# Throw-away 512-column matmuls ahead of each tile's scores in three attention stages of a fused decoder kernel

## What is computed

```
x = x + tanh(g_xattn[0]) * decayed_context_product(layernorm(x), ctx)
x = x + tanh(g_ffn[0])   * moe_16_experts(layernorm(x))
x = x + tanh(g_xattn[1]) * attention_16_heads(layernorm(x), ctx)         # turn 1
x = x + tanh(g_ffn[1])   * moe_8_experts(layernorm(x))
x = x + tanh(g_xattn[2]) * attention_16_heads(layernorm(x), ctx, mask)   # turn 3
x = x + tanh(g_ffn[2])   * moe_lora_4_experts(layernorm(x))
x = x + tanh(g_xattn[3]) * perceiver_attention(ctx, layernorm(x))
x = x + tanh(g_ffn[3])   * block(layernorm(x))      # block = self-attention (turn 6), norm, moe
```

## Time and profile before

| | us |
|---|---|
| median of 3 runs | 2141.67 (2140.36 to 2143.73) |
| profiled execution, its own time | 2139.78 |
| span of the profiled execution | 2137.9 |
| TensorE busy (matmuls) | 1587.1 (74% of the span) |
| VectorE busy | 1389.8 (65%) |
| ScalarE busy | 842.2 (39%) |
| GpSimd busy | 500.2 (23%) |
| mean granted TensorE clock | 0.852 of full speed |

### The profile page before, as it was taken

The page is one execution under the profiler, slowest core; times in us unless marked ns, Lnnn a source line. Parts: engine busy times, 40 slices in busy tenths (PEclk is TensorE's granted clock), DMA queues, the critical chain, the costliest instruction groups (busy, mean ns, idle before and its releaser), DMA issues. The chain is left out here.

```text
span 2137.9 us, 28891 instructions
## 1 busy us (share of the span) xinstructions
PE 1587.1 (74%) x10054; PEld 1060.8 (50%) x10054; DVE 1389.8 (65%) x4779; ACT 842.2 (39%) x1809; POOL 500.2 (23%) x347
## 2 busy tenths in 40 slices
PE   5779476876787847797777965788687794669768
PEld 3546333664554624465554542356464463336636
DVE  5459866747547976665645797565664589657466
ACT  0325033852334413484333421367233261237623
POOL 1305501420031530240011351143002055023200
PEclk7879778987988969898888987899788797689979
DMA  7000000000000000000000000000000000000000
GB/s 266 1 1 1 1 1 0 1 12 2 7 1 1 1 0 1 0 1 13 1 7 1 1 1 1 1 1 1 13 1 7 1 1 0 1 0 1 1 13 6
DMA packets 16833, 19.78 MB, mean 9 GB/s; under 512 B 3344, under 2 KB 15384, under 8 KB 16156
## 3 DMA queue, kind: packets, MB, share of 16 engines
q1 hardware_dynamic: 16672, 17.75, 2.5%
HBM read 16.70 MB, written 1.05 MB: 8 GB/s over the span
## 5 line engine op out<-in xcount | busy, mean ns | idle before, releaser
L305 PE MATMUL bank<-w_x,consts 128*128 128x512 f32 x168 | 107.1, 789 | 69.3 <-issue 69.3
L322 ACT COPY xnT<-bank 128x256 f32<-128x256 f32 x56 | 20.8, 372 | 320.9 <-PE bank L316 320.5
L931 PEld LDWEIGHTS bank<-w_f1d,work 128*128 128x128 f32 x1024 | 127.0, 203 | 36.6 <-issue 25.1
L931 PE MATMUL bank<-w_f1d,work 128*128 128x129 f32 x1024 | 129.0, 288 | 20.4 <-DVE work L1046 20.4
L456 PE MATMUL bank<-consts,work 128*128 128x128 f32 x384 | 72.2, 349 | 85.0 <-ACT work L506 84.7
L972 ACT ACTIVATE work<-bank,w_f 128x512 f32<-128x512 f32 x128 | 87.0, 686 | 112.4 <-PE bank L919 112.2
L919 PE MATMUL bank<-xnT,w_f 128*128 128x512 f32 x256 | 127.4, 644 | 3.3 <-ACT work L972 3.3
L456 PEld LDWEIGHTS bank<-consts,work 128*128 128x128 f32 x384 | 57.4, 180 | 133.9 <-ACT work L506 131.9
L1375 ACT ACTIVATE work<-work,small 128x128 f32<-128x128 f32 x256 | 99.9, 407 | 0.3
L305 PEld LDWEIGHTS bank<-w_x,consts 128*128 128x128 f32 x168 | 40.5, 258 | 111.9 <-issue 111.9
L1460 POOL TENSOR_TENSOR work<-work,small 128x1024 f32<-128x1024 f32 x32 | 60.7, 1896 | 147.3 <-DVE small L1520 147.3
(11 more groups left out here) (283 smaller groups left out, 4184.7 us busy)
## 6 DMA issues: line engine op xcount, KB each, us to landing
w_f<-in_f_dram SPq DMA_DIRECT2D x1, 2616.0 KB
w_f<-in_f_dram SPq DMA_DIRECT2D x1, 2180.0 KB
w_x<-in_x_dram SPq DMA_DIRECT2D x1, 2115.0 KB
w_l<-in_l_dram SPq DMA_DIRECT2D x1, 2088.5 KB, 21.5
w_f1d<-in_f1d_dram SPq DMA_DIRECT2D x4, 512.0 KB
work<-in_x_dram SPq DMA_DIRECT2D x5, 256.0 KB, 3.0
work<-in_ctx_dram SPq DMA_DIRECT2D x5, 256.0 KB, 3.4
out_dram<-x SPq DMA_DIRECT2D x4, 256.0 KB, 2.3
```

The costliest lines, as they stand in the source:

```text
L305: pe.matmul(bank[:, :], ident, w_x1[:, 0:512], start=True, stop=True)
L931: pe.matmul(zb(t)[:, 0:129], hT[e % 2][:, c, t * P:(t + 1) * P], w_f1d[:, c, e, :], start=(c == 0), stop=(c == 3))
```

## The change

`scores(t)` gets a call of the existing helper `keep_clock`, behind its waits and ahead of its four matmuls: two throw-away statements for t = 0, one for each of t = 1, 2, 3. They write all 512 columns of the first bank that the scores then overwrite. Nothing else changes.

```
--- before.py
+++ after.py
@@ -437,6 +437,7 @@
                         pe.wait_ge(kv.kx_ready, t + 1)
                         if t >= 2:
                             pe.wait_ge(s_ready, t - 1)
+                        keep_clock(pe, banks[2 * (t % 2)], 2 if t == 0 else 1)
                         for b in range(PAIR):
                             for g in range(HEADS // GROUP):
                                 r = slice(64 * g, 64 * g + 64)
```

## The result

The changed kernel takes 2155.29 us (median of 8 runs, 2150.0 to 2159.72) against 2144.16 for the kernel before in the same sessions (8 runs, 2140.36 to 2148.94): ratio 1.0049, 95% interval 1.0034 to 1.0065, or +10.5 us. The forecast was +20, with a range from +4 to +38, so the median lies in the range, at about half of the central value. The profiled execution took 2156.16 us, 16.4 more than that of before, so it shows somewhat more than the typical cost.

A forecast was written before the change was run, and what follows sets the result against it. No engine is full; a serial chain through TensorE, ScalarE and VectorE bounds attention stages. Turns 1, 3 and 6 at 8 + 8 + 3, plus about 1 for weight loads, gave +20 us: 2160 profiled, 2162 median, range 2146 to 2180.

The forecast's parts named there:

- The fill of tile 0 is on the serial chain: Attention stages: tile 0's two statements always push back its scores, costing 1.7 us (upper clock) to 3.4 (lower).
- The 1 us for weight loads: All attention stages: about 1 us in total for the first weight load of each fill's identity.
- Turn 1, tile 0, +2.9 in three of four stages: Turn 1: fill of 3.4 us less 0.5 back from faster scores, net +2.9; block 1 +1.7.
- 3.4 us where the clock is down: Turn 1, tile 0: two statements take 3.4 us at the lower clock, 1.7 at the upper.
- a shift hardly later: Sign against the forecast: if tile 0's shift came hardly later, the fill would not be on the path.
- Turn 1, tile 2, a gain of 1.0: Turn 1, shift 0 to shift 2: 7.96 us becomes 6.9 at the upper clock, in three stages; +0.5 in block 1.
- Turn 1, the tail: Turn 1, tile 3 after shift 2: transposes, mix, fill and scores fit in 3.9 us at the upper clock, so nothing.
- rival (a): Clock stays up from tile 0's scores to the last mix: -8 us and some 2 more, 2132; chance 0.09.
- Turn 3, +8: Four stages at 2.1: tile 0's fill +2.7, the 0.59 us idle before tile 2 goes (-0.6), tail 0.
- Turn 6, +3: Four stages at 0.7: tile 0 +0.5 after 1.2 us of slack, tile 3 +0.2.
- Rival (b): Fills run at the lower clock and raise nothing: +50 us, 2192; chance 0.08.
- Rival (c): It washes out: turn 6 gains 1 to 2 us a stage, turns 1 and 3 pay 1; within 0.2%; chance 0.06.

The follow-up runs named there:

- gap_more: Kernel before plus throw-away statements inside exponentials waits (tiles 0, 2, 3; in turn 6 also tile 1), bank wait first: ratio 0.9848, 2110.59 us.
- gap_all: Kernel before plus statements inside exponentials waits, bank wait first: two at tile 0 (three in turn 6), one each at tiles 2 and 3: ratio 0.9885.
- t0_only: Changed kernel with only the two statements ahead of tile 0's scores kept; ratio 1.0053 against the kernel before, +11.3 us.
- t0_double: Changed kernel with four statements instead of two ahead of tile 0's scores; ratio 1.0118 against the kernel before, +25.3 us.
- gap_and_t0: Kernel before plus two statements inside the wait for tile 0's exponentials and two ahead of tile 0's scores; ratio 1.0043, +9.2 us.

## Why the prediction was right, and where it was not

- **The fill of tile 0 is on the serial chain: right.** VectorE's wait before tile 0 in turn 3 grew by 2.7 to 2.8 us in three blocks and by 3.7 in block 3 (+2.7 forecast); alone the fill costs 11.3 us, beside a hidden fill 25. The 1 us for weight loads had no row behind it and no run isolates it; in turn 1, block 1 the fill holds the scores back by 1.91 us (113.89 to 115.80), some 0.2 more than two statements at 0.86.
- **Turn 1, tile 0, +2.9 in three of four stages: wrong in this execution.** The step "3.4 us where the clock is down" took the level at the query projection from the trace of before. It was up in three of four blocks afterwards, so the fill took 1.98 us, and in block 2 tile 0's shift came hardly later (4.94 us after the projection's start for 4.60). The prediction had named a shift hardly later as a sign that the fill is not on the path; it is not such a sign here, since block 1, at the same level before and after, shows +1.92 (+1.7 forecast), and block 3, the one block in which the fill ran at the lower level (3.78 us for two statements), +2.95.
- **Turn 1, tile 2, a gain of 1.0: wrong, the sign too.** I assumed that a clock just raised would last until the transposes and scores of tile 2. In three of four blocks it fell there, and shift 2 waited about 3.05 us, not 1.3. It was up for the transposes, as foretold, but not for fill and scores. In block 3, where tile 0's fill ran at the lower level as the forecast assumed, the wait was 1.41 us: the step held where its condition did.
- **Turn 1, the tail: a term that the forecast put at nothing.** VectorE's waits before tile 0 grew by 5.7 us over the four blocks and those before tile 2 by 2.3; the waits ahead of tile 2's reciprocal shrank by 4.8, which the prediction had in rival (a) alone (1.6 a stage). These three make +3.2 of the +3.3 us measured, where the forecast had +8.
- **Turn 3, +8: the profile has +10.6.** The idle time of 0.5 to 0.9 us before tile 2 did not go; it became 1.6 in three blocks, for the same reason: the wait of 3.45 us let the clock fall, and the fill of tile 2 then ran at the lower level. The tails in exchange were at the upper level, tile 3's transposes at 1.09 us in all four blocks where two had 1.97.
- **Turn 6, +3: +5.0.** Tile 0's idle entry is there (0.73 and 0.56 us in two blocks, none in the others); the loss at tile 3 (0.5 to 0.8 us idle) was booked too low. So the sum of the profiled attention stages, +18.8 for a forecast of 20, is near by turns that miss in opposite directions, which is luck.
- **What was mis-sized.** I booked +24 for tile 0's fill and some -4 for those of tiles 1 to 3, mostly from tile 2. By the medians tile 0's is worth +11.3 by itself and +21 beside the others, and the others -10.7 by themselves and -0.8 beside it, so which term carries the error depends on the order in which they are taken. The profiled attention stages stand near both terms (+22.3 and -3.8), and where the rest of the median's difference goes is open. One thing is clear: tile 1's fill, which I had put down as "nothing", gives nearly all that the later ones give by themselves (-9.2 of -10.7). I was right that its cost is hidden and missed what it wins: it stands just ahead of a wait.
- **Rival (a), the clock stays up and the kernel is faster,** did not happen here, but its mechanism is real: gap_more has it. My argument against it held, "nothing fills the gaps themselves"; put into the gaps, the fills win 1.5%. The section "HAM oscillation — how this bites in real kernels" of the Trainium skill ("TensorE: Matmul & The Clock Gate") says that gaps bring the slow clock back. The traces agree: behind the wait of 3.45 us in turn 3 the transposes took 1.92 us, the lower level. The same page's 215.7 ns for 512 bf16 columns did not hold as the price of a float32 statement: two of them took 1.98 us at the upper level.
- **Rival (b)** would have needed the lower level throughout; in turn 3 tile 0's scores ran at the upper level in three of four blocks (1.09 us for 1.98), as the earlier trace rows suggested. **Rival (c)** would have needed a median within 0.2%; the interval begins at 0.34%.

The mechanism of the cost was right, the net was put at twice the measured size. The single profiled execution, +16.4, lies nearer to the forecast than the median of the runs does, mostly because the profiled execution of the kernel before (2139.78) was 4.4 us faster than the median it is compared with (2144.16).

## What to carry to other kernels

Throw-away matmuls are worth what their place is worth. Behind a wait on a serial chain they cost about their length (here 25 us for two statements in 12 stages, beside a hidden fill); inside a wait that TensorE has anyway, in a bank that is free, they cost nothing that shows here and can hold the clock for the work behind it (32.5 us won). Find the waits in which the granted clock falls, and fill those, before filling what comes after them; a higher mean clock (0.868 for 0.852 here) is no sign of a faster kernel, and the profiled execution of gap_all, with the same 0.868, was 42 us faster than that of the change.

## What was not expected of the hardware

The level at a given place of a stage differs between blocks of one execution and between kernels that are the same up to there: the query projection of turn 1 ran at the upper level in one block of four before and in three of four after, with nothing changed in front of it within the stage. The launch's first attention stage began its query projection at 112.01 us in one profiled execution and at 114.52 in the other, ahead of the first changed instruction of either. The kernel before itself spreads from 2129.2 to 2149.03 us over 28 runs of one session, while gap_more, in which the clock was up at all first transposes of its profile, spreads over 2.9 us in 5 runs; gap_all, with the clock up at all of them too, spreads over 11.8 in 6. The five stages that no edit touches took between 1525 and 1538 us in sum in the profiled executions of the kernels here. The lowest sums belong to kernels with tile 0's fill (1525.7 in t0_only, 1525.9 in t0_double, 1528.6 in gap_and_t0), but the change has 1536.9, as the kernel before has, so one profile cannot place a difference of ten microseconds; and matmuls of 64 columns kept 14.4 us of the gain of 512-column ones, for a reason that the runs leave open.
